# A tokenizer, attention and expert layer on one core: zero products ahead of the first patches, a two-row bias, a new order of the token tiles, and their last step on GpSimd

## The reference, cut to what matters

```python
x = layernorm(x, ln1_g, ln1_b)
x = jnp.einsum('bhwp,pd->bhwd', x, W) + bias
x = layernorm(x, ln2_g, ln2_b)
x = x.reshape(b, HP * HP, DIM) + pe[None]
...
h = jnp.concatenate([h, txt], axis=1)
h = h + _L0_attn_ref(_layernorm(h, axis=-1), wq, wk, wv)
h = h + _L0_ffn_ref(_layernorm(h, axis=-1), shared_up, shared_down, routed_up, routed_down, router_w)
```

## Time and profile before

| | us |
|---|---|
| median of 3 runs (330.55 to 332.09) | 330.74 |
| the profiled execution | 329.75 |
| its span, first to last instruction | 327.9 |
| PE busy | 298.2 (91%) |
| POOL busy | 205.8 (63%) |
| DVE busy | 160.9 (49%) |
| ACT busy | 145.2 (44%) |

### The profile page before, as it was taken

One profiled execution on the slowest core, in us unless ns is written; L12 is line 12 of the kernel. 1 busy time (PEld: TensorE's weight loads), 2 busy tenths in 40 slices (PEclk: granted clock), 3 DMA queues, 4 the chain that ended last, 5 costly groups with the idle time before them and its releaser, 6 DMA issues.

```text
span 327.9 us, 6674 instructions
## 1 busy us (share of the span) xinstructions
PE 298.2 (91%) x2058; PEld 269.8 (82%) x2059; DVE 160.9 (49%) x409; ACT 145.2 (44%) x325; POOL 205.8 (63%) x164
## 2 busy tenths in 40 slices
PE   0899879898999999897999999999999999999970
PEld 0477869787998899895988999899989998899870
DVE  3778888987837786642332333224332333233220
ACT  3696233658777273432434433343334433353300
POOL 3276480557870004759898899899887898345541
PEclk9999999997999999999999999999999999999997
DMA  7996112014434321674455426533552532324532
GB/s 233 320 212 208 35 49 118 13 59 161 160 118 170 83 92 51 184 250 151 146 192 179 142 67 190 182 58 160 160 171 80 123 59 35 61 22 48 60 39 27
DMA packets 21925, 39.91 MB, mean 122 GB/s; under 512 B 2913, under 2 KB 18226, under 8 KB 19602
## 3 DMA queue, kind: packets, MB, share of 16 engines
q0 software_dynamic: 7456, 25.43, 28.9%
q1 hardware_dynamic: 14162, 14.03, 13.8%
q10 hardware_dynamic: 288, 0.20, 0.2%
HBM read 28.84 MB, written 6.93 MB: 109 GB/s over the span
## 4 chain that ended last, share of the span: by engine, by line
PE 39%; POOL 16%; DVE 12%; DMA 12%; issue 11%; ACT 4%; POOLq 3%; SPq 0%; DVEq 0%; ACTq 0%
DMA out_tokens<-xy_all,dest 11%; PE ps L984 8%; PE ps L986 7%; PE ps L985 7%; PE ps L1033 7%; POOL ring L441 6%; PE ps L852 4%; POOL ring L440 3%; POOL out_tokens L588 3%; POOLq L585 2%; PE ps L883 2%; PE ps L1104 1%; DVE ps L1277 1%; DVE qk L1276 1%; PE ps L954 1%
## 5 line engine op out<-in xcount | busy, mean ns | idle before, releaser
L441 POOL TENSOR_TENSOR ring<-stage,ring 128x512 fp32r<-128x512 f32 (+2 forms) x30 | 76.2, 2540 | 2.5
L1571 DVE TENSOR_TENSOR hgT<-ps,hgT 128x512 fp32r<-128x512 f32 x50 | 32.2, 686 | 72.3 <-ACT hgT L842 72.3
L984 PE MATMUL ps<-ring,hgT 128*128 x200 | 58.0, 290 | 2.1 <-DVE xy_all L1577 1.5
L588 POOL DMA_INDIRECT out_tokens<-xy_all,dest x25 | 39.5, 1581 | 27.6 <-DMA out_tokens<-xy_all,dest 18.0
L985 PE MATMUL ps<-ring,hgT 128*128 x200 | 55.9, 279 | 0.0
L986 PE MATMUL ps<-ring,hgT 128*128 x200 | 55.9, 279 | 0.0
L834 ACT ACTIVATE hg<-ps 128x512 f32<-128x512 f32 x50 | 30.0, 599 | 47.6 <-PE ps L986 47.6
L578 POOL DMA_INDIRECT xy_all<-normalized_tokens,dest x25 | 24.9, 994 | 36.8 <-DVE dest L1534 29.5
L984 PE MATMUL ps<-ring,xgT 128*128 x100 | 41.4, 414 | 1.1 <-issue 0.6
L984 PEld LDWEIGHTS ps<-ring,hgT 128*128 128x128 f32 x200 | 37.6, 188 | 2.5 <-issue 2.5
L985 PE MATMUL ps<-ring,xgT 128*128 x100 | 39.4, 394 | 0.0
(11 more groups left out here) (192 smaller groups left out, 590.3 us busy)
## 6 DMA issues: line engine op xcount, KB each, us to landing
stage<-in_w_up POOLq DMA_DIRECT2D x9, 1024.0 KB, 5.5
stage<-in_w_dn POOLq DMA_DIRECT2D x9, 1024.0 KB, 5.6
xg<-xy_all SPq DMA_DIRECT2D x25, 128.0 KB, 2.0
xp<-in_patches SPq DMA_DIRECT2D x4, 384.0 KB, 7.8
normalized_tokens<-hn SPq DMA_DIRECT2D x4, 276.0 KB
residual_tokens<-h SPq DMA_DIRECT2D x4, 276.0 KB
ring<-in_tok_w SPq DMA_DIRECT2D x1, 768.0 KB, 7.5
base<-residual_tokens SPq DMA_DIRECT2D x2, 384.0 KB, 4.8
```

What stands on the lines that cost most here:

```text
L441: return nc.gpsimd.tensor_tensor(lo, stage[:, part, c0:c1], hi.bitcast(F32), ALU.subtract)
L588: pool.indirect_dma_start(out, bass.IndirectOffsetOnAxis(ap=dest[:, t:t + 1].bitcast(U32), axis=0), xy_all[:, t, :], None, compute_op=ALU. ...
L984: nc.tensor.matmul(o, a[0], b[0], start=n == 0, stop=False)
L1571: v.tensor_tensor(hgT[:, c, 1, 4 * half:4 * half + 4, :], ps[:, turned_bank + half, :].rearrange("p (k t) -> p k t", k=4), hgT[:, c, 0, 4 ...
```

## The change

Six things are done.

1. DVE sets `zero` to zeros as its first instruction (before: behind the last `attention_low`). PE multiplies zeros nine times ahead of the first transposes and three times between those of tile 0 and of tile 1 (`idle_products`). The results are written over later.
2. The bias comes as two rows, an upper and a lower part, made by POOL in three small operations (`bias_halves`, ahead of `tok_root(2)`), and is multiplied by two rows of -1 in the rounded float32 form, one record, as the last matmul of each product.
3. Half of the pieces of tile 1, too, are scaled by DVE instead of ACT.
4. `tok_end` is taken from DVE and given to POOL, as a multiplication and an addition with a wait between them.
5. On POOL the waits for `a_norm_in` are gone.
6. All four engines get a new order of the same steps. PE does the products earlier against the transposes of text and attention, and ACT makes the copy of the values of group 0 ahead of the normalization of tile 4.

```diff
@@ constants and buffers @@
+IDLE_FIRST, IDLE_SECOND = 9, 3
+        minus = sb("minus", [2, P], F32R, where=signing)
+        bias_high = sb("bias_high", [2, D], F32R, where=halving)
+        bias_parts = sb("bias_parts", [2, D], F32R, where=halving)
-        biasr = sb("biasr", [1, D], where=tok)
+        biasr = sb("biasr", [2, D], where=tok)
@@ sync @@
             load_patches(0, 2)
+            sp.dma_start(biasr[:, :], tok_bias.partition_broadcast(2)).then_inc(bias_in, 16)
             sp.dma_start(tw[:, :, :], tok_w.rearrange("(k p) d -> p k d", p=P)).then_inc(tok_w_in, 16)
-            sp.dma_start(biasr[:, :], tok_bias).then_inc(bias_in, 16)
             load_patches(2, 3)
@@ gpsimd @@
+            nc.gpsimd.memset(minus[:, :].bitcast(F32), -1.0)
+            def bias_halves():
+
+                pool.wait_ge(bias_in, 16)
+                pool.wait_ge(first_in, 32)
+                link(nc.gpsimd.tensor_scalar(bias_high[:, :], biasr[:, :], 1.0, 0.0, ALU.mult, ALU.add))
+                link(nc.gpsimd.tensor_scalar(bias_high[:, :], bias_high[:, :].bitcast(F32), ident[0:2, 1:2], None, ALU.mult))
+                nc.gpsimd.tensor_tensor(bias_parts[:, :], bias_high[:, :].bitcast(F32), biasr[:, :],
+                                        ALU.subtract).then_inc(bias_ready, 1)
+            def tok_end(i):
+                pool.wait_ge(t_gain, i + 1)
+                if i == 0:
+                    pool.wait_ge(cls_in, 32)
+                r, n = AROWS[i], NPT + i
+                pool.wait_ge(t_rstd2, i + 1)
+                link(nc.gpsimd.tensor_scalar(tt[0:r, i, :], tt[0:r, i, :], trs[0:r, n:n + 1], None, ALU.mult))
+                pool.wait_ge(pe_ready, i + 1)
+                nc.gpsimd.tensor_tensor(tt[0:r, i, :], tt[0:r, i, :], pe[0:r, i, :], ALU.add).then_inc(t_done, 1)
             tok_root(1)
+            bias_halves()
             tok_root(2)
...
             tok_root2(0)
+            tok_end(0)
+            tok_root(4)
             load_weights(0)
-            tok_root(4)
             place_rows_of(1)
+            tok_root2(1)
+            tok_end(1)
             attention_root(0)
-            pool.wait_ge(a_norm_in, 1)
+            place_rows_of(2)
+            attention_root(1)
+            tok_root2(2)
+            tok_end(2)
             attention_weights()
-            tok_root2(1)
+            attention_root(2)
             load_weights(1)
-            attention_root(1)
-            pool.wait_ge(a_norm_in, 2)
-            place_rows_of(2)
             place_rows_of(3)
-            tok_root2(2)
-            attention_root(2)
-            pool.wait_ge(a_norm_in, 3)
+            tok_root2(3)
+            tok_end(3)
             place_rows_of(4)
-            tok_root2(3)
+            tok_root2(4)
             attention_root(3)
-            tok_root2(4)
+            tok_end(4)
             attention_root(4)
@@ scalar, the last part of its order @@
             attention_norm(2)
             attention_copy(5)
+            attention_copy(6)
             attention_norm(3)
-            attention_copy(6)
             attention_copy(7)
+            attention_values(0)
             attention_norm(4)
-            attention_values(0)
             attention_copy(8)
@@ tensor @@
                 o = ps[0:r, 4 + i % 2, 0:D]
+                te.wait_ge(t_aff, i + 1)
+                if i < 2:
+                    te.wait_ge(t_aff_half, i + 1)
                 if i == 0:
-                    te.wait_ge(bias_in, 16)
-                nc.tensor.matmul(o, ones[0:1, 0:r], biasr[:, :], start=True, stop=False)
-                te.wait_ge(t_aff, i + 1)
-                if i == 0:
-                    te.wait_ge(t_aff_half, 1)
                     te.wait_ge(tok_w_in, 16)
                 for c in range(KP):
-                    last = nc.tensor.matmul(o, xT[:, i % 2, c, 0:r], tw[:, c, :], start=False, stop=c == KP - 1)
-                last.then_inc(t_mm, 1)
+                    nc.tensor.matmul(o, xT[:, i % 2, c, 0:r], tw[:, c, :], start=c == 0, stop=False)
+                if i == 0:
+                    te.wait_ge(bias_ready, 1)
+                nc.tensor.matmul(o, minus[:, 0:r], bias_parts[:, :], start=False, stop=True).then_inc(t_mm, 1)
+
+            def idle_products(n):
+
+                for _ in range(n):
+                    nc.tensor.matmul(ps[:, 5, 0:D], zero[:, 0:P], zero[:, :], start=True, stop=True)
@@ vector @@
-            def tok_end(i):
-                dve.wait_ge(t_rstd2, i + 1)
-                dve.wait_ge(t_gain, i + 1)
-                dve.wait_ge(pe_ready, i + 1)
-                if i == 0:
-                    dve.wait_ge(cls_in, 32)
-                r, n = AROWS[i], NPT + i
-                v.scalar_tensor_tensor(out=tt[0:r, i, :], in0=tt[0:r, i, :], scalar=trs[0:r, n:n + 1], in1=pe[0:r, i, :],
-                                       op0=ALU.mult, op1=ALU.add).then_inc(t_done, 1)
+            v.memset(zero[:, :], 0.0).then_inc(empty_row, 1)
             tok_stats(0)
...
             tok_stats(2)
+            tok_turned(1)
             tok_shift(2)
```

68 lines of the change are left out of this document (35 added, 33 removed).

## The result

The changed kernel takes 335.24 us (median of 4 runs, 334.37 to 337.86); the kernel before took 331.41 beside it (4 runs, 330.55 to 332.18). The ratio is 1.018, with a 95% interval of 1.012 to 1.024. The profiled execution took 335.11 us, its span is 333.2 (before: 327.9).

What follows compares the result with a forecast made beforehand. No engine bounds the first 45 us; a chain of waits up to group 0's scores sets the end. Scores 0.9 us later plus collisions of 1.0 give +1.8; 329.75 + 1.8 + 0.99 for the median: 332.5 us, range 329.2 to 335.0.

Steps and rivals of the forecast that it cites:

- The start: Up to the first product: zero products raise PE's clock, product 0 is over by 14, stats2(0) at 17.1, not 17.6.
- the warm clock: PE's high clock level at product 0: gains 0.5 us, because DVE waited only 0.69 us for that product.
- The price of one tile end on POOL: Multiply 0.40, link 0.08 and addition 0.72 make 1.20 us on POOL, in place of 0.48 on DVE.
- The bound of 1.7: Upper bound in us for one tile end on POOL, from 0.62 and an addition of 1.07 beside DVE.
- The POOL chain: POOL becomes the later engine: attention_root(0) at 24.0, front(2) at 27.6, front(3) at 35.4, where it was 34.34.
- The tail: From front(3) to the scores of group 0: 9.55 us, scores at 44.9, 0.9 us later without collisions.
- Collisions: With POOL's waits gone, bias(0) and bias(2) on DVE meet POOL's position rows: 1.0 us, bounds 0 and 2.
- Rival 1, the clock falls in the new hole: PE idles over 3 us ahead of the values and its clock falls: 1.5 us more, 334.0; chance 0.20.
- the forecast case: POOL's longer tile ends and the collisions delay the scores: +1.8 us, from +1.0 to +2.6; chance 0.40.
- The end moves as much as the scores: After 45 us the same work follows in order, so the end moves as much as the first attention group.
- No change: Rival: POOL's tile end costs 0.8, front(3) starts between 34.8 and 35.4: -0.1 to +0.9, 331.1; chance 0.20.
- faster: Rival: POOL is never waited for, front(3) at 33.3 (starting by 34.5 decides): -1.9, 328.8; chance 0.15.

Runs made afterwards that it cites:

- e10: Changed kernel with GpSimd's multiply of all five tile ends in the two-operation form (times root, plus 0.0): 332.44 us, ratio 1.011.
- e2: Changed kernel without its twelve products of zeros: ratio 1.019 to the kernel before.
- e9: Changed kernel with a different form of GpSimd's tile-end multiply in each token tile, for durations alone: one execution, 333.46 us.
- the three pairs: GpSimd's waits for the biases of tiles 0 and 2 put back: on the changed kernel (1.013), with two-operation multiply (1.006), with tile end on VectorE (1.001).
- e8: Kernel before with the tile end alone moved to GpSimd, in two operations: 336.41 us, ratio 1.023.
- the three profiles with fills: Changed kernel with zero products in TensorE's holes: alone (1.027), with tile end on VectorE (1.002), and with bias(3) first as well (1.011).
- e6: Changed kernel with twelve more zero products in TensorE's holes ahead of the transposes of tiles 6, 7 and 8: 337.87 us, ratio 1.027.
- e4: Changed kernel with attention_bias(3) put ahead of attention_front(4) on VectorE: 334.8 us, ratio 1.014.
- e14: Changed kernel with the tile end on VectorE as one operation and GpSimd's waits for the biases of tiles 0 and 2 back: ratio 1.001.
- e5: Changed kernel with the constant 1.0 in place of the root in GpSimd's tile-end multiply: 335.01 us, ratio 1.017.
- e12: Changed kernel with the tile end on VectorE as one operation and eight zero products in TensorE's holes: 330.41 us, ratio 1.002.

## Why the prediction was right and wrong, step by step

From stats2(0) to the scores the forecast has 28.8 us (45.9 - 17.1), and it took 32.94. Of the 4.1 us, 1.55 are the clock and some 2.2 the slow form of the multiply (1.30 that e10 gives back, and 0.9 that e10 loses again to its own collision, an estimate); the last 0.4 no run shows.

- **The start** (products at the high level, product 0 over by 14, stats2(0) at 17.1): right in its times; 16.68, and DVE's wait for product 0 gone. But the 0.5 us that it gave to the warm clock aren't the warm clock's: without zero products (e2) DVE doesn't wait for product 0 either.
- **The price of one tile end on POOL, 1.20 us: wrong, and the step that failed.** It took an operation of 256 columns with one input from a row of another form, at 0.40. That form takes 0.40 to 0.48 indeed (e9); the change writes the one-operation form, 0.94. It also left out the wait of 0.17 for POOL's own root. It is 1.91 to 1.96 in place of 1.20, four times, and 1.74 for tile 4, whose root is long done. The bound of 1.7 was too low as well, since it allowed for a collision and not for a slower form. The form alone was worth 1.30 in the token tiles (e10), with the new collision there taken off.
- **The POOL chain**: right in its order and in who waits, 1.3 us early at attention_root(0) (6.9 us from stats2(0), really 8.2) and 2.5 at front(2), most of which the price makes. A residue stays with the price put right: e10 starts front(3) 20.6 us after stats2(0), where 18.3 were forecast without collisions and 19.3 with them. Of that 1.3, 0.85 is root2(1) waiting behind the collision of tile 4's shift, which the prediction didn't have and the changed kernel hasn't either. The four waits of 0.17 for POOL's own root could make the rest; no run shows it.
- **The tail**, 9.55 us from front(3) to the scores: 11.47 after, 9.46 in e10. The sum of its steps was right, and the two terms above it were the end of tile 4 (1.74 in place of 1.24) and the clock (1.55); they give 2.05, and 1.92 was measured.
- **Collisions**, 1.0 us: right; 0.98, 0.94 and 0.78 in the three pairs. That a small VectorE operation with two SBUF inputs is held until GpSimd's pass is over is what the Trainium skill (SBUF — State Buffer, section "SBUF: two separate sides") states, and the trace agrees: 0.15 alone; beside the addition of 24.89, 0.72 long, 0.68, and both end at 25.6.
- **Rival 1, the clock falls in the new hole** (chance 0.20): it came together with the forecast case, at 1.55 us, where 1.5 was its price. A hole of the size that it named doesn't bring the fall by itself: e10 has one of 3.11 us ahead of the values and no fall there, and in the changed kernel the clock was low from 37 to 40 already, ahead of the hole of 2.32. The sum was short because forecast and rival were priced as alternatives, and both happened.
- **The end moves as much as the scores**: nearly. 5.6 became 5.3. The 1.8 more in the shared expert go with the fall at 125 (e2, without it, has 60.8 there against 62.9). Of the 2.1 less ahead of it, some 1.5 go with the missing fall near 75 (e8, in the old order and without it, has 41.8 against 43.3).
- **No change, faster**: both out; front(3) at 38.15 is far past their 34.5 and 35.4.

With the multiply in its fast form the kernel takes 332.44 us, and the forecast was 332.5. That agreement is partly luck: e10 has 0.6 us more at the scores than forecast, its profile has the old fall at 75, and its ratio is 1.011 where the forecast's is 1.005.

What stays open: why falls of the clock come where they do, why the three profiles with fills have one at 155, why the median of e6 is so high, and why a median at times moves less than the stages (e4, e14).

## What to carry to other kernels

Price a moved operation from a row of the very same form, with the same count of operations in it, on the engine it goes to; where there is none, let the bound include a factor of two. An operation that leaves a fast engine in one instruction and arrives on a slow one in two is paid in every link of a serial chain (here 1.9 us for 0.48, and 1.45 in its best form), and an idle share of the engine that receives it is no argument. Where two mechanisms can happen together, add them; only what excludes each other may be priced as rivals. And look for collisions again after each change of a duration: the shorter multiply of e10 put a small VectorE operation under a long GpSimd one, and lost there what it had saved.

## What was not expected of the hardware

- GpSimd's tensor_scalar over 256 f32 columns: 0.94 us with one operation and a scalar in memory, 0.87 to 0.90 with one operation and a constant; with a second operation (plus 0.0) 0.48 and 0.40. A tensor-by-tensor multiply with the scalar broadcast took 0.61, under the one-operation form too.
- On GpSimd the multiply behind its own root started 0.17 to 0.20 us after the root's end; the addition behind the multiply only 0.08 after.
- A small VectorE operation with two SBUF inputs (128x1, 0.15 us alone) took 0.56 to 0.68 beside a GpSimd pass of 0.6 to 0.7, and up to 1.36 in other places (e9).
- A low clock is not tied to a long hole: the values of group 0 ran at the high level behind 3.11 us of idle (e10), and in large part at the low level behind 2.32 (after). A fall ahead of the very end cost 1.1 (e10, near 77: 42.85 us from the scores to the shared expert against 41.74 in e5) to 2.7 us (e12, near 157), and the three kernels with added zero products in the attention stage, and no other, had one at about 155 us in their profiles.
